# A PixArt block pair on one core: context stores ahead of the key diagonals, two memsets behind the keys, and LayerNorm statistics of the next stage some rounds earlier

## What is computed

```
def ada_ln(x, c, W_ss, b_ss):
    h = (x - mean(x)) / sqrt(var(x) + eps)
    scale, bias = split(silu(c) @ W_ss + b_ss, 2)
    return (1 + scale)[:, None, :] * h + bias[:, None, :]
# L0
q = heads(ada_ln(x, cond, ...) @ Wq + bq);  k, v = heads(ada_ln(ctx, cond, ...) @ Wkv + bkv)
x = x + softmax(q @ k.T / sqrt(32)) @ v @ Wp + bp
# L1
shift_a, scale_a, gate_a, shift_m, scale_m, gate_m = split(silu(cond) @ W_mod + b_mod, 6)
q, k, v = split(modulate(ln(x), shift_a, scale_a) @ W_qkv + b_qkv, 3)
x = x + gate_a * (softmax(q @ k.T * scale) @ v @ W_proj + b_proj)
q = ln(x) @ W_qc + b_qc;  k, v = split(ln(ctx) @ W_kvc + b_kvc, 2)
x = x + softmax(q @ k.T * scale) @ v @ W_cproj + b_cproj
x = x + gate_m * (gelu(modulate(ln(x), shift_m, scale_m) @ W_mlp1 + b_mlp1) @ W_mlp2 + b_mlp2)
```

## Time and profile before

| | |
|---|---|
| median of 3 executions | 2470.44 us (2468.13 to 2471.92) |
| profiled execution, device time | 2474.41 us |
| its span, first to last instruction | 2472.6 us |
| PE busy | 2372.6 us, 96% |
| PEld busy | 1666.6 us, 67% |
| DVE busy | 1378.9 us, 56% |
| ACT busy | 1016.3 us, 41% |
| POOL busy | 607.2 us, 25% |
| packets of SP's queue, share of the DMA engines' span | 50.2% |

### The profile page before, as it was taken

The page is one execution under the profiler, slowest core; times in us unless marked ns, Lnnn a source line. Parts: engine busy times, 40 slices in busy tenths (PEclk is TensorE's granted clock), DMA queues, the critical chain, the costliest instruction groups (busy, mean ns, idle before and its releaser), DMA issues.

```text
span 2472.6 us, 32517 instructions
## 1 busy us (share of the span) xinstructions
PE 2372.6 (96%) x12056; PEld 1666.6 (67%) x12056; DVE 1378.9 (56%) x2471; ACT 1016.3 (41%) x1799; POOL 607.2 (25%) x509
## 2 busy tenths in 40 slices
PE   6889999999999999999998899999999999999999
PEld 5666667688786344444444567776788888888887
DVE  6566665744565877778776477666542222322221
ACT  3344544523233655555554344444442233233232
POOL 2002111200001766767766311212101101101100
PEclk9999999999999999999999999999999999999999
DMA  7697897645745554555651688877421110110110
GB/s 245 195 247 208 218 247 207 206 166 192 222 178 167 146 126 120 133 146 140 153 149 58 168 226 215 222 202 210 149 62 46 60 57 4 60 60 1 60 43 18
DMA packets 261324, 354.20 MB, mean 143 GB/s; under 512 B 61027, under 2 KB 109243, under 8 KB 261166
## 3 DMA queue, kind: packets, MB, share of 16 engines
q1 hardware_dynamic: 259998, 348.27, 50.2%
q0 software_dynamic: 1168, 3.85, 0.4%
HBM read 233.78 MB, written 116.69 MB: 142 GB/s over the span
## 4 chain that ended last, share of the span: by engine, by line
PE 81%; DVE 8%; ACT 4%; DMA 3%; issue 3%; SPq 1%; POOL 0%; ACTq 0%; DVEq 0%; POOLq 0%
PE banks L403 43%; PE banks L2263 14%; PE banks L1961 5%; PE banks L1983 4%; PE banks L1940 4%; PE banks L2003 3%; PE banks L1362 2%; PE banks L361 2%; PE banks L1376 2%; PE banks L1383 2%; DVE negated_max L1875 1%; DVE negated_max L1261 1%; DMA q_parts_self<-out_parts 1%; DVE heads_float L1901 1%; ACT self_exponentials L2047 1%
## 5 line engine op out<-in xcount | busy, mean ns | idle before, releaser
L2047 ACT ACTIVATE self_exponentials<-banks 128x512 f32<-128x512 f32 x512 | 285.6, 594 | 269.3 <-PE banks L1961 112.8
L1875 DVE TENSOR_REDUCE negated_max<-banks 128x1 f32<-128x512 f32 x512 | 330.2, 677 | 92.1 <-PE banks L1940 90.8
L1840 POOL TENSOR_TENSOR self_exponentials<-self_exponentials,self_exponentials 128x512 f32<-128x512 f32 x252 | 320.0, 1299 | 166.9 <-ACT self_exponentials L2047 166.9
L2263 PE MATMUL banks<-mlp_w_down_hi,out_parts 128*128 128x512 f32 x1024 | 333.8, 389 | 0.1
L344 POOL TENSOR_SCALAR norm_rstd<-norm_mean_var 128x4 f32<-128x4 f32 x32 | 8.0, 250 | 1301.1 <-DVE norm_mean_var L323 1301.1
L2220 DVE TENSOR_TENSOR out_parts<-wide,out_parts 128x512 fp32r<-128x512 f32 x128 | 92.9, 726 | 370.7 <-ACT out_parts L2292 370.7
L2282 ACT ACTIVATE wide<-banks,bias_columns 128x512 f32<-128x512 f32 x128 | 88.3, 690 | 426.0 <-PE banks L403 426.0
L1961 PE MATMUL banks<-self_query_stack,self_key_stack 98*128 98x512 f32 x512 | 232.3, 457 | 10.1 <-ACT self_exponentials L2047 7.2
L1961 PEld LDWEIGHTS banks<-self_query_stack,self_key_stack 98*128 98x128 f32 x512 | 96.5, 189 | 193.8 <-ACT self_exponentials L2047 159.2
L2263 PEld LDWEIGHTS banks<-mlp_w_down_hi,out_parts 128*128 128x128 f32 x1024 | 192.2, 188 | 40.5 <-DVE cross_last_x_rows L1305 0.5
L1940 PE MATMUL banks<-self_key_stack,self_query_stack 96*128 96x512 f32 x512 | 205.7, 405 | 9.1 <-DVE negated_max L1875 9.1
(11 more groups left out here) (209 smaller groups left out, 5232.7 us busy)
## 6 DMA issues: line engine op xcount, KB each, us to landing
L_query_stack<-q_parts_L SPq DMA_DIRECT2D x96, 256.0 KB, 4.9
norm_x<-x SPq DMA_DIRECT2D x24, 1024.0 KB, 7.9
self_query_stack<-q_parts_self SPq DMA_DIRECT2D x96, 256.0 KB, 4.0
self_key_stack<-k_parts_self SPq DMA_DIRECT2D x96, 256.0 KB, 6.3
cross_query_stack<-q_parts_cross SPq DMA_DIRECT2D x96, 256.0 KB, 5.0
x_rows<-x SPq DMA_DIRECT2D x23, 1024.0 KB, 5.9
x<-x_rows SPq DMA_DIRECT2D x22, 1024.0 KB, 5.4
q_parts_L<-out_parts SPq DMA_DIRECT2D x32, 512.0 KB, 4.8
```

The source lines that it names most:

```text
L1840: e.tensor_tensor(self.p[kt - 1][:, h, :], self.p[kt - 1][:, h, :], self.p[kt][:, h, :], ALU.add).then_inc(self.paired.sem, 1)
L1875: e.tensor_reduce(k.nm[n % 2][:, h * NT + t:h * NT + t + 1], k.bank[:, self.max_banks.of["max", i], :], AX_X, ALU.max, negate=True).then_i ...
L2047: e.activation(self.p[kt][:, h, :], k.bank[:, self.scores.of["score", i], :], ACT.Exp, scale=SCALE).then_inc(self.exp.sem, 1)
L2263: mm = e.matmul(bank, l, w, start=j == 0 and q == 0, stop=j == JC - 1 and q == 2)
```

## The change

The change moves instructions and alters none. The steps that it moves are these:

- In `Prepare.run` more steps of L0 are taken beside the value tiles, and the last two tiles are placed elsewhere: tile 3 stands ahead of the first maxima, tile 4 ahead of the third.
- In `CrossAttention.run` for L0 the two memsets of ones stand together behind the context keys. `load_diagonals(0)` and `load_keys(0)` come one round later, behind the stores of value tiles 0 and 1. The normalisation of batch 1 starts ahead of the first maxima, and these four tiles run without query matmuls between them. `load_diagonals(1)` comes right behind the third query.
- For cross, one empty round stands ahead of `load_values(0)`, and self-attention takes ten steps of cross instead of nine.
- `ahead` becomes (1, 3, 2, 4, 0, 0, 2, 2) for L0 and (1, 3, 2, 4, 0, 0, 4, 0) for cross: the same number of steps, begun two rounds earlier.

```diff
-        yield from braid(some(1, following), some(3, values))
-        yield from braid(some(15, following), after(8, slowly(3, values)))
+        yield from braid(some(6, following), some(3, values))
+        yield from braid(some(17, following), after(2, slowly(10, values)))
...
-            if n == 0 or not self.layer:
-                s.ones(n)
+            if n == 0 and self.layer:
+                s.ones(0)
         if not self.layer:
+            s.ones(0)
+            s.ones(1)
+        yield
+        if not self.layer:
+            normalising = quarter(2)
+            next(normalising)
+            yield
             s.load_diagonals(0)
             s.load_keys(0)
-        yield
...
-            yield from braid(s.query(2), s.maxima(0), quarter(2))
+            yield from normalising
+            asking = s.query(2)
+            yield from some(3, asking)
+            yield from braid(s.maxima(0), after(3, asking))
+            s.load_diagonals(1)
...
-        s.load_values(0)
-        next(quarter(self.LEAD))
-        s.load_diagonals(1)
+        if self.layer:
+            next(quarter(self.LEAD))
+            yield
+            s.load_values(0)
+            s.load_diagonals(1)
+        else:
+            s.load_values(0)
+            next(quarter(self.LEAD))
...
-        yield from braid(s.project(B - 1), some(9, following))
+        yield from braid(s.project(B - 1), some(10, following))
...
-        l0 = CrossAttention(k, w, "L0", 0, (1, 4, 4, 1, 2, 2), 6, ...
+        l0 = CrossAttention(k, w, "L0", 0, (1, 3, 2, 4, 0, 0, 2, 2), 6, ...
-        cross = CrossAttention(k, w, "cross", 1, (1, 4, 4, 1, 4, 0), 3, ...
+        cross = CrossAttention(k, w, "cross", 1, (1, 3, 2, 4, 0, 0, 4, 0), 3, ...
```

More of the change, by code:

```diff
@@ L2320, in __init__ @@
         prepare = Prepare(k, w)
-        l0 = CrossAttention(k, w, "L0", 0, (1, 4, 4, 1, 2, 2), 6, (4, 5), (4, 5), a["x"], None, k.x1, 1e-5, ("L0q_scale", "L0q_shift"), prepare.mod_made(3),
+        l0 = CrossAttention(k, w, "L0", 0, (1, 3, 2, 4, 0, 0, 2, 2), 6, (4, 5), (4, 5), a["x"], None, k.x1, 1e-5, ("L0q_scale", "L0q_shift"), prepare.mod_made(3),
                             a["L0_xcond_Wq"], "L0_bq", a["L0_xcond_Wp"], a["L0_xcond_bp"],
@@ L2326, in __init__ @@
         attention = SelfAttention(k, w, k.x1, k.x2, a["L1_xcond_W_proj"])
-        cross = CrossAttention(k, w, "cross", 1, (1, 4, 4, 1, 4, 0), 3, (3, 4), (2, 3), k.x2, attention.x_stored, k.x3, 1e-6, None, None,
+        cross = CrossAttention(k, w, "cross", 1, (1, 3, 2, 4, 0, 0, 4, 0), 3, (3, 4), (2, 3), k.x2, attention.x_stored, k.x3, 1e-6, None, None,
                                a["L1_xcond_W_qc"], "L1_b_qc", a["L1_xcond_W_cproj"], a["L1_xcond_b_cproj"],
```

## The result

The changed kernel takes **2457.12 us** (median of five, 2455.63 to 2461.26) where the kernel before takes 2470.44 (median of five, 2468.13 to 2472.25). The ratio is 0.9948, with a 95% interval of 0.9936 to 0.9959: 13.3 us, or 0.5%, faster. The forecast was 2455.9, a gain of 14.5.

The account below looks back on a forecast made before the run. The prediction took PE, busy 2372.6 of 2472.6 us, to bound the kernel. Savings of 1.1 + 2.3 + 1.5 + 4.0 + 4.4 + 0.6 + 0.6 = 14.5 took the median 2470.44 to 2455.9, range 2446 to 2465.

Parts of the forecast that it names:

- the second diagonals: L0, near 137.91 us: PE's 2.64 wait for diagonals and the low clock behind it go, 4.0 us saved.
- the start of cross: Near 1420.96 us: PE's 3.87 wait for diagonals shrinks to 0.7, and 1.2 of clock is won: 4.4 us saved.
- the memset: Start of L0: memset of ones moves behind the keys, so DVE's key parts and PE come sooner, 1.1 us saved.
- the first maxima: L0, near 106 us: waits of 0.67 and 2.43 become 0.8, 2.3 us saved, plus 1.5 of low clock.
- The ends: Ends of L0 and cross: earlier normalisation cuts the 1.6 wait for negated_max by 1.0, less 0.4 for late reduces: 0.6 each.
- The new wait of 0.7: Start of cross: PE's remaining wait for diagonals, the middle taken between none and 1.4 us.
- the second case: Ends of L0 and cross: PE returns to 2.4 GHz, 2 x 2.8 = 5.6 us more won, 2450.3; chance 0.17.
- One of its signs of being wrong: A DVE wait for norm_x in front of a reduce near 407 or 1678 us; no size given.
- new waits: Rival: second diagonals cost 3.8, first come 1.5 late, norm_x loads delay reduces: 6.9 us lost, 2462.8; chance 0.18.
- the third rival: Starts of L0 and cross: PE meets the next late thing, so little beyond the memset is won, 2469; chance 0.08.
- the slower case: Ends of L0 and cross: norm_x loads push query_stack fetches late, 29.6 us in all, 2485; chance 0.05.
- The one rule against the change: DMA ring order: two value stores ahead delay L0's first diagonals, landing in 4.4 instead of 1.9 us; sum 13.0.

Follow-up runs that it names:

- b_late: Kernel before the change plus only a wait on POOL that delays the last batch's bias in L0 and cross until PE's last scores: 0.9982 of the kernel before.
- u_stores: Changed kernel with L0's first diagonals and first key stack issued ahead of the stores of value tiles 0 and 1 again: 0.9955 of the kernel before.
- u_diag1: Changed kernel with L0's second diagonals issued behind the 1 MB load of norm_x again: 0.9947 of the kernel before.
- u_ends: Changed kernel with the old numbers of steps at the ends of L0 and cross: 0.9950 of the kernel before.
- u_ends_late: Changed kernel with old step numbers at both ends, plus POOL's last-batch bias delayed until PE's last scores: 0.9930 of the kernel before.

## Why the prediction was right

The forecast of the total was 1.2 us off, and a good part of that is luck. Two terms hold by their mechanism, the second diagonals and the start of cross, 8.4 of the 14.5, and so does the memset. The term of the first maxima, 3.8, was read from waits and a clock that the same code doesn't have in `b_late`'s execution. The ends were wrong in both directions. And the two profiles that are compared are both slow ones, the one before by 4.0 over its median and the changed one by 4.1; the first lost time at the start of L0 and the second 4.5 in `Qkv`.

- **Memset:** forecast 1.1, measured 1.5 in DVE's chain, and 2.5 by the ratios, which can't tell this from nothing. The mechanism held: back-to-back work of DVE ahead of the keys. But the sign that was named for it, 2.5 of idle at the first key parts, came as 0.66, since some 2 us of the 3.57 were a late load of weights.
- **First maxima:** forecast 2.3 + 1.5 = 3.8. Against the profile of before, 95 to 130 us is 2.7 shorter; against `b_late`'s, 0.0. The waits that it names fell from 3.1 to 0.3, but 1.25 + 1.05 stand behind them instead. The wait of DVE for the store went as forecast, and with that order restored PE's comes back by only 0.6. The low clock, 1.5, is absent in `b_late` as well, so it isn't shown that it went with the change. The sum had errors of its own here: nine query matmuls take 2.1 (98.01 to 100.07), not 3.4, and value tile 3 takes 2.8 (to 102.84), not 0.6, for it is a full tile of 12 matmuls.
- **Second diagonals:** forecast 4.0, measured 3.8 to 4.3 in the profiles of the eleven kernels with it, and 0.3 and -0.3 in the two without. The bounds of 0 and 3.8 for the eight issues came out at 0.
- **Start of cross:** forecast 4.4, measured 5.3, and 4.0 by the ratios when undone. The new wait of 0.7 was the middle between a landing of 1.9 and one of 4.4; it took 3.0, and PE found the diagonals there. The 1.2 of clock in this term isn't certain: `u_stores` and `u_diag1` win only 3.8 here, since their clock is 0.72 over six us of this place without any wait for diagonals.
- **The ends:** forecast 0.6 each, measured -0.2 and 0.8, and 0.5 in all when undone, all of it within what equal code differs by. Two terms were mis-sized. The reduces' lateness was counted as 0.4 with a bound of 1.2: the load took 9.1 to land, where the earlier trace rows gave 7.4, and PE's waits of 0.38 and 0.88 became 1.8 of lead lost (8.8 ahead, then 7.0). And the clock, which the forecast left low, came back at the end of L0 (1.00 over 436 to 442, where 0.50 stood), as the second case had it; it did so there in each of the five kernels with these numbers and POOL as it was. That second case failed at its next step: its 2.8 were given back as waits for exponentials, through DVE slowed by POOL. The prediction never asked what DVE and ACT do behind the last reduces. One of its signs of being wrong did come: DVE waits 3.65 for `norm_x` in front of a reduce at 401.67 (and 1.52 at 1665.85).
- **The rivals:** new waits came at the ends and at the start of L0, where PE met the next late thing much as the third rival had it (ACT's `wide`, 1.25). No wait for `query_stack` appeared, so the slower case had no ground. The one rule against the change didn't come about: the first diagonals of L0 landed in 1.9 with two value stores in front, as without them, and those of cross in 3.0, 1.1 more than alone, which cost PE nothing.

## What to carry over

A bubble that closes near the end of a stage only moves PE forward to the next engine in line: look at what that engine does in the ten microseconds behind the bubble before counting the gain. Where POOL and DVE work beside each other on SBUF, compare the mean of one DVE instruction inside and outside POOL's busy stretches; a wait on POOL that moves its work is worth 6.9 us here in the changed kernel and 4.4 in the one before, against 13.3 for the whole change. And with terms of 1 to 4 us in 2460, undo one at a time and read the lead at the same matmul in both traces, since medians of whole runs can't tell them apart. Before a wait becomes a term of a sum, look for it in a second execution of the same code: here 4.6 us of one profile's waits and low clock were not in the other.

## What the runs showed that I had not expected

**The low clock doesn't belong to one wait.** In the prediction each low stretch stood behind one gap and was to go with it. In `u_ends` a wait of 1.6 us at the end of L0 is followed by 1.2 GHz. In `u_ends_late` the same wait of 1.6 is there and the clock stays at 2.4 GHz over the same 6 us:

```profile
436.00:442.00 6.00, 5.05 (x31) 2.54 (x31) 4.04 (x8) 4.25 (x10) 0.12 (x1) 1.00 1.04 359
```

And the changed kernel has low stretches where the one before has none, for one 0.77 over 1375 to 1381 us, in code that the change doesn't touch, while 0.66 over 106 to 111 us of the kernel before is 1.00 in `b_late`. Whether a gap is followed by the low clock varied from kernel to kernel with the same gap. Its total varied too: PE's busy time is 2368.5 us in the changed kernel and 2361.2 in `u_ends_late`, with the same matmuls (their ends are modelled in a profile). I had taken the clock terms as certain; they are chances.

**A DVE instruction of 0.69 us takes up to 1.8 beside POOL.** The difference, 1.1, is less than one of POOL's additions (1.28 to 1.29 us each from 180 to 367 us of the changed kernel), as it would be if DVE waited for the end of the one under way. POOL pays too: its eight additions at the end of L0 take 1.28 to 1.75 each. And who starts first seems to decide. At 462.12 us of the kernel before, a DVE instruction of this kind starts together with an addition of POOL (462.11): it takes its 0.66, and the addition 1.83.
